# One order changed in the latent attention steps: the narrow product ahead of the third tile, the small pieces ahead of the last rotation

## The reference, cut to what matters

```python
q_hk = (hidden_q @ Wq.T).reshape(Bv, Sv, H, K)
q_big = _apply_rope(jnp.einsum('bshk,hkq->bshq', q_hk, w_kc_q), sin_q, cos_q)   # 192 wide, rotated
q_r = jnp.einsum('bshq,hqr->bhsr', q_big, W_qr)
k_r = jnp.einsum('bld,hdr->bhlr', kv_r, W_kr)
attn = jax.nn.softmax(jnp.einsum('bhsr,bhlr->bhsl', q_r, k_r), axis=-1)
ctx_c = jnp.einsum('bhsl,bld->bhsd', attn, kv_r)
# then w_kc_kv and Wo, added to x; then a layer norm and a feed-forward
# whose activations are quantised in blocks of 32 (the "front" does this for x)
```

## Time and profile before

| | |
|---|---|
| median of 3 runs | 898.3 us (895.77 to 899.1) |
| the profiled execution | 895.51 us |
| its span, first to last instruction | 893.5 us |
| mean granted TensorE clock | 0.962 |
| PE busy | 795.0 us, 89% of the span |
| DVE busy | 644.8 us, 72% |
| POOL busy | 464.7 us, 52% |
| ACT busy | 400.3 us, 45% |
| latent steps: first matmul of step 0, of step 31 | 378.03 us, 753.26 us |

### The profile page before, as it was taken

The page is one execution under the profiler, slowest core; times in us unless marked ns, Lnnn a source line. Parts: engine busy times, 40 slices in busy tenths (PEclk is TensorE's granted clock), DMA queues, the critical chain, the costliest instruction groups (busy, mean ns, idle before and its releaser), DMA issues. The chain is left out here.

```text
span 893.5 us, 14677 instructions
## 1 busy us (share of the span) xinstructions
PE 795.0 (89%) x4792; PEld 562.9 (63%) x4792; DVE 644.8 (72%) x1162; ACT 400.3 (45%) x1074; POOL 464.7 (52%) x479
## 2 busy tenths in 40 slices
PE   3999999578999998789999999999999999757675
PEld 2545455246877787567877777777777777524443
DVE  4898898375887888667456666786677668479884
ACT  2678888432232232215444444444454444533443
POOL 3555555314676766434353455455555454345674
PEclk9999999787999999989999999999999999987999
DMA  9100000030000010222200000000000000000001
GB/s 270 70 1 0 0 0 1 1 134 22 19 23 32 18 53 0 79 75 95 96 1 1 1 1 2 1 1 1 1 1 2 1 1 1 1 1 8 22 30 36
DMA packets 8761, 24.63 MB, mean 28 GB/s; under 512 B 1711, under 2 KB 4143, under 8 KB 8087
## 3 DMA queue, kind: packets, MB, share of 16 engines
q1 hardware_dynamic: 8154, 23.81, 8.0%
q10 hardware_dynamic: 549, 0.08, 0.1%
HBM read 21.79 MB, written 2.10 MB: 27 GB/s over the span
## 5 line engine op out<-in xcount | busy, mean ns | idle before, releaser
L1445 POOL TENSOR_TENSOR p<-p,l_inverse 128x512 f32<-128x512 f32 x64 | 67.0, 1047 | 195.1 <-DVE l_inverse L1404 195.1
L1146 PE MATMUL ps<-l_yt,a 128*128 128x512 f32 x576 | 150.0, 406 | 0.2 <-DVE l_yt L1347 0.2
L1146 PEld LDWEIGHTS ps<-l_yt,a 128*128 128x128 f32 x576 | 104.5, 190 | 31.7 <-DVE turned L1382 7.6
L1279 ACT ACTIVATE p<-ps,l_negmax 128x128 f32<-128x128 f32 x256 | 91.3, 384 | 50.3 <-DVE l_negmax L1373 50.3
L1382 DVE TENSOR_TENSOR turned<-ps,rope 128x1024 f32<-128x1024 f32 x64 | 78.1, 1220 | 47.4 <-PE ps L1146 47.4
L766 PE MATMUL ps<-yt_experts,wsplit 128*128 (+1 forms) x384 | 99.9, 411 | 4.6 <-DVE h L855 2.8
L395 DVE TENSOR_REDUCE negmax<-ps 128x4 f32<-128x512 f32 x128 | 85.3, 687 | 11.2 <-PE ps L244 9.4
L1160 PE MATMUL ps<-q,b 128*128 128x512 f32 x192 | 89.3, 602 | 2.6 <-DVE cs L1410 2.6
L766 PEld LDWEIGHTS ps<-yt_experts,wsplit 128*128 128x128 f32 x384 | 72.4, 195 | 22.8 <-issue 4.2
L326 ACT ACTIVATE pt<-ps 128x512 f32<-128x512 f32 x128 | 72.9, 597 | 8.0 <-PE ps L264 3.9
L1296 ACT ACTIVATE qs<-ps 128x512 f32<-128x512 f32 x32 | 19.1, 598 | 120.5 <-PE ps L1160 120.5
(11 more groups left out here) (187 smaller groups left out, 1638.3 us busy)
## 6 DMA issues: line engine op xcount, KB each, us to landing
wide<-in_wide SPq DMA_DIRECT2D x8, 768.0 KB, 4.4
mx_raw<-in_mx SPq DMA_DIRECT2D x8, 384.0 KB, 3.2
x<-in_x SPq DMA_DIRECT2D x4, 512.0 KB, 8.7
ctx_t<-in_ctx_t SPq DMA_DIRECT2D x1, 2048.0 KB, 7.6
narrow<-in_narrow SPq DMA_DIRECT2D x8, 256.0 KB, 3.0
out<-x SPq DMA_DIRECT2D x16, 128.0 KB, 1.7
ktraw<-in_ctx_rows SPq DMA_DIRECT2D x1, 1248.0 KB
wraw<-in_gate SPq DMA_DIRECT2D x1, 1024.0 KB, 18.1
```

The lines of the kernel that those rows point to most:

```text
L1146: out = pe.matmul(tile_ps[t % 2], a[i][:, pa, kin, k * 128:(k + 1) * 128], yt[j % 2][:, py, kin, :, :].rearrange("p b s -> p (b s)"), star ...
L1279: t = act.activation(p[:, head, s, :], s_ps[head][:, s * S:(s + 1) * S], ACT.Exp, bias=negmax[:, head, s:s + 1], accum_out=total[:, head, ...
L1445: pool.tensor_tensor(p[:, head, :, :], p[:, head, :, :], spread(inverse[:, head, :], 2, S), ALU.mult).then_inc(normed[head], 1)
```

## The change

On TensorE `tile(n, 2)` moves behind `narrow_product(n - 1)` and `spare(n, 1)`. On ScalarE the copy of spare place 0 moves ahead of `exponential(n - 2, 1)`. On VectorE the splits of spare places 0 and 1, the last statistics of step 0, `normalise` and the pieces of the front move ahead of `rotate_last(n)`, and five of the six pieces (with the deviations on GpSimd) come one step later; `multiply` stays in its step and `divide` comes to it.

```diff
@@ TensorE
                 tile(n, 0)
                 tile(n, 1)
                 spare(n, 0)
-                tile(n, 2)
                 narrow_product(n - 1)
                 spare(n, 1)
+                tile(n, 2)
                 turn_p(n - 2, 0)
@@ ScalarE
                 exponential(n - 2, 0)
                 keep_context(n - 3)
+                spare(n, 0)
                 exponential(n - 2, 1)
-                spare(n, 0)
                 keep_narrow(n - 1)
@@ VectorE
                 rotate_both(n, 1)
+                spare(n, 0)
                 invert(n - 2, 1)
-                spare(n, 0)
-                rotate_last(n)
                 spare(n, 1)
-                spare(n, 2)
                 if n == 0:
                     last_statistics()
                 if n % PAIRS == 1 and n // PAIRS < GROUPS - 1:
                     normalise(n // PAIRS + 1)
-                for k, part in ((2, f.add), (3, f.statistics), (5, f.normalise), (6, f.scales), (7, f.divide), (8, f.multiply)):
+                for k, part in ((3, f.add), (4, f.statistics), (6, f.normalise), (7, f.scales), (8, f.divide), (8, f.multiply)):
                     if front_in(n, k) is not None:
                         part(dve, m, front_in(n, k))
+                rotate_last(n)
+                spare(n, 2)
@@ GpSimd
-                if front_in(n, 3) is not None:
-                    f.deviations(pool, m, front_in(n, 3))
+                if front_in(n, 4) is not None:
+                    f.deviations(pool, m, front_in(n, 4))
```

## The result

The changed kernel takes **916.14 us** as the median of 4 runs (915.28 to 920.41), against 897.03 us for the kernel before (894.2 to 899.1 in 4 runs). The ratio is 1.0225, with a 95% interval from 1.0192 to 1.0258: slower by 19 us, where +20 and 918 us were forecast. The profiled execution took 915.82 us, with a span of 913.8 us against 893.5: +20.3.

The account below looks back on a forecast made before the run. TensorE was taken to set the latent steps' time. The terms 14.4 + 1.7 + 0.9 + 1.1 + 1.4 + 0.7 - 0.3 = 19.9, say +20, on 898.3 gave 918 us, range 910 to 925.

Parts of the forecast that it names:

- What bounds the kernel: In the latent steps TensorE sets the time; what it loses in a step, no other engine gives back.
- The hole in an empty step: In 20 steps without spare work in place 0, the narrow product waits for the context's split: +0.72 us each, +14.4.
- Steps 3 to 7, 15, 17, 23, 25: Spare work fills part of the hole: +0.27 each in 3 to 6, +0.58 in 7, 15, 23, +0.43 in 17, 25.
- the 1.47 us for a tile behind spare work: In steps 3 to 7, 15 and 23, the time charged for tile 2 when it follows spare work.
- The first steps: Later splits and moved waits in steps 0, 1 and 2: +1.4, +0.7 and -0.3 us.
- What I had at nothing: Last rotation and front pieces on VectorE, front's add, ScalarE's copy: no cost, maxima 0.3 us late in the worst step.
- the worst step: Step with the front's division and multiplication together, 4.6 us on VectorE: last rotation ends at 11.6 us.
- The last steps: ScalarE's copy delays the second exponential by at most 1.7 us; the second transposes have over 2 us to spare.
- Rival 1: The narrow product does not wait, as the split ends before 2.86 us into the step: 896 or 894 us; 4%.
- Rival 2: The clock falls in TensorE's holes: +16, 934 us, in every fifth step, or +51, 969, in each of 20; 7%.
- Rival 3: VectorE sets the period where the front works, with the last rotation behind it: 15 us more, 933 us; 4%.
- Rival 4: TensorE's restart after the wait is cheap and the first steps come out even: +14, 912 us; 12%.

Follow-up runs that it names:

- e1: The kernel before with TensorE's part of the change alone, tile 2 moved behind the narrow product and spare place 1: 921.92 us, ratio 1.0293.
- e4: The kernel before with VectorE's split of the context moved ahead of the first rotation: 917.58 us, ratio 1.0244.
- e5: The changed kernel with an extra VectorE reduction that nobody reads ahead of each context split: 935.22 us, ratio 1.0447.
- e2: The changed kernel with TensorE's order of before, keeping the new order of VectorE, ScalarE and GpSimd: 902.52 us, ratio 1.0088.
- e6: The kernel before with an extra VectorE reduction that nobody reads ahead of each context split: 899.31 us, ratio 1.0044.
- e7: The changed kernel with ScalarE's copy of the front's result put back behind the second exponential: 912.73 us, ratio 1.0195.
- e3: The changed kernel with VectorE's split of the context moved ahead of the first rotation: 904.92 us, ratio to the kernel before 1.0076.

## Why the prediction was right, point by point

**What bounds the kernel.** Right: TensorE passed every hole on in full, in e1, e4 and e5 as in the change.

**The hole in an empty step.** Right to the second decimal. The narrow product was to start at 3.72 and take 4.04 us together with tile 2; in step 16 it starts at 589.90 - 586.17 = 3.73 and the transposes come 593.94 - 589.90 = 4.04 later. The period grew by 0.71 for a forecast of 0.72, and the steps 8 to 30 took 15.34 us more. The restart had been read from a single wait in step 32, the only place where this wait was bare, and it held in all these steps.

**Steps 3 to 7, 15, 17, 23, 25.** The mechanism was right; the size was off by 0.08 in the steps with work in place 1 (0.19 for 0.27, 0.48 and 0.52 for 0.58). The step that failed is the 1.47 us for a tile behind spare work. In step 4 the time from the first matmul of place 1 to the transposes grew from 0.77 us to 2.17 with the tile in between, so the tile cost 1.40: part of its slow start stands in the 0.77 already and was counted twice.

**The first steps.** Signs right, sizes too large: +0.99 for +1.4, +0.26 for +0.7, -0.11 for -0.3. In step 0 the narrow weights did start at 389.37 (forecast 389.4) and their wait was the forecast one:

```profile
388.89 0.42 DVE L1342 TENSOR_TENSOR wc<-ps,wc 128x256 fp32r<-128x256 f32 x1
...
389.37 1.47 PE L1092 MATMUL ps<-narrow 128*128 128x128 f32 x6 [3.22 <-DVE wc L1342]
```

What differs is mostly the clock: these matmuls and the two tiles behind them took 1.47 and 4.18 us where they had taken 1.65 and 4.61; the tiles explain nearly all of the 0.44 in step 1, the matmuls 0.19 of step 0's 0.4, and another 0.16 is that step 0 began that much later. e2 has the same 12.30 in step 0, which puts this cost on VectorE's order alone. The sizes are soft all the same: e6, whose steps 0 and 1 have the orders of before, took 10.19 and 12.03 us there at a clock of 1.00, against 11.31 and 13.65 at 0.85 and 0.87 in the kernel before.

**What I had at nothing.** The last rotation and the front's pieces cost nothing in the changed kernel, and in step 16 as forecast: the maxima are 0.3 late and the context's copy is over 2.06 us into step 17. But the worst step is not that one. In step 17 VectorE waits for the second exponential, which the front's copy on ScalarE delays (the normalisation behind it starts 6.07 us into the step, and 4.71 in e7), and then normalises the next group's rows in 4.04 us, so that the last rotation ends at 12.10 and not at 11.6 at worst. Step 17, VectorE; then step 18, which starts at 610.79, the copy and the split:

```profile
604.46 0.18 DVE L1404 RECIPROCAL l_inverse<-l_total 128x4 f32<-128x4 f32 x1 [1.26 <-ACT p L1279]
604.56 4.04 DVE L1332 TENSOR_SCALAR l_y<-x,mv,rstd 128x256 f32<-128x256 f32 x4
...
608.51 2.08 DVE L1394 TENSOR_TENSOR turned<-ps,rope 128x512 f32<-128x512 f32 x3
```

```profile
612.74 0.61 ACT L1288 ACTIVATE cs<-ps 128x512 fp32r<-128x512 f32 x1
```

```profile
613.71 0.66 DVE L1410 TENSOR_TENSOR cs<-ps,cs 128x512 fp32r<-128x512 f32 x1
```

The copy is over at 2.56, the rotation ahead of the split ends at 2.9, and the split still ends at 3.58: a margin of some 0.36 us. e3 and e2 show what happens without it: with a step shorter by 0.7 to 0.9 us the pieces cost up to 0.8 us in the step behind them.

**The last steps: missed.** "it delays that exponential by at most 1.7 us and the second transposes have over 2 us to spare" fails in step 33, where TensorE has no tiles: 0.9 us (e7). I had not followed the order into the steps that drain the pipeline. Of the +4.47 us from step 31 on, 0.7 is step 31's hole and 0.9 this copy. The remaining 2.9 is a spell at half clock. From the second transposes of step 33 to the feed-forward TensorE does the same in both kernels; it took 5.86 us before (780.91 to 786.77) and 8.98 now (800.16 to 809.14), 3.1 more, and step 32's narrow product was 0.3 shorter. The mean clock from step 31's first matmul to the feed-forward was 0.95 before and 0.82 now. The last twelve matmuls of the projection in step 34, before and after:

```profile
784.75 1.69 PE L1183 MATMUL ps<-wc,cs 128*128 128x256 f32 x12 [1.41 <-DVE cs L1410]
```

```profile
805.89 2.93 PE L1183 MATMUL ps<-wc,cs 128*128 128x256 f32 x12 [1.42 <-DVE cs L1410]
```

In the kernel before, such a spell came later, in the feed-forward, which now had a clock of 0.92 instead of 0.87 and took 2.1 us less. The last steps missed 3.75 us of the sum. The feed-forward's 2.1 and the terms that were too large (1.5 together, 0.7 of it in steps 0 to 2) took nearly as much back, which is why the sum of 19.9 met a measured 20.3 in the span. That part of the agreement is luck.

**The rivals.** Rival 1 is out: 25 waits. Rival 2 is out for the latent steps: the stretch of 164 us above has 13 of the holes and a clock of 1.00. What the Trainium skill says of short idle times between groups ("TensorE: Matmul & The Clock Gate", section "A second HAM failure mode: psum-queue depth-cycling") does not show here for holes of 0.86 us in 12.3, nor for the 1.5 us in every step of e5, where PE was busy for 137.4 of 152 us from 635 us on and the clock was 1.00 too. Rival 3 is out for the change but not for e3. Rival 4's cheap restart is out.

## What to carry to other kernels

When an instruction is moved forward on the bounding engine, list all its waits and ask for each when it becomes true in the step, not whether it was ever waited for: a wait that costs nothing may be one that was just covered. If two results of a second engine are consumed by the first in some order, produce them in that order; if the orders differ, the first result's duration, less the slack that the other had, is paid in every step (here 0.69 of the split's 0.69 us in e4, and 0.94 with the restart for the rotation's 1.23 in the changed kernel, against e3). And do not stop at the steady step: the first and last steps have other covers.

## What the runs showed of the hardware that I had not expected

- Spells at half clock move between stages: from the feed-forward, whose instructions did not change, into the last latent steps, and out of the first ones. A few us of difference between kernels can be that alone, as the +2.9 in the last latent steps here; the -2.1 in the feed-forward goes with a clock of 0.92 for 0.87. What started each spell just there was not tried.
- Four normalisations of 128x256 elements on VectorE took 1.37 us together in step 1, where GpSimd stood idle, and 4.02 us in step 17 of e3, where GpSimd was normalising the softmax and adding without a pause. The last three of the four took 1.13, 1.38 and 1.37 us and GpSimd's three beside them 1.12, 1.34 and 1.33, so each waits as it seems for one of GpSimd's to end. The kernel before has it too, with 3.40 us in step 17. That is a factor of up to 3 that no duration from one place shows, and I had priced each piece from one place. The Trainium skill's "GPSIMD Engine Reference", section "1. Specifications", says that GpSimd shares its SBUF interfaces with VectorE and contends with VectorE's instructions in a two-port mode or with two inputs in SBUF. The two rows, of step 1 in the changed kernel and of step 17 in e3, agree with such a contention; in which mode these instructions ran, no row shows.

```profile
399.82 1.37 DVE L1332 TENSOR_SCALAR l_y<-x,mv,rstd 128x256 f32<-128x256 f32 x4
```

```profile
598.05 4.02 DVE L1332 TENSOR_SCALAR l_y<-x,mv,rstd 128x256 f32<-128x256 f32 x4
```
